# Laying the product rows of a state-space scan eight partitions apart, loaded in twelve transfers of 16 rows per chunk

## The reference

```python
xc = silu(conv(x_z)); dt = clip(softplus(xc @ dt_W + dt_b), 0.001, 0.1)
Bp = xc @ B_W; Cp = xc @ C_W; A = -exp(A_log)
def step(h, ins):
    x_t, dt_t, B_t, C_t = ins
    dA = exp(dt_t[..., None] * A)
    h = dA * h + dt_t[..., None] * B_t[:, None, :] * x_t[..., None]
    y_t = einsum('ben,bn->be', h, C_t)
```

## Time and profile before

| | us |
|---|---|
| median of 3 runs | 1180.5 (1174.55 to 1181.07) |
| profiled execution | 1172.6 |
| its span, first to last instruction | 1170.8 |
| staging part, then scan | to about 176, then to the end |
| TensorE / VectorE / ScalarE / GpSimd busy | 1018.2 / 937.3 / 910.6 / 851.4 |
| mean granted clock of TensorE | 0.905 of full |

### The profile page before, as it was taken

One profiled execution on the slowest core, in us unless ns is written; L12 is line 12 of the kernel. 1 busy time (PEld: TensorE's weight loads), 2 busy tenths in 40 slices (PEclk: granted clock), 3 DMA queues, 4 the chain that ended last, 5 costly groups with the idle time before them and its releaser, 6 DMA issues.

```text
span 1170.8 us, 27899 instructions
## 1 busy us (share of the span) xinstructions
PE 1018.2 (87%) x8006; PEld 433.0 (37%) x8006; DVE 937.3 (80%) x2127; ACT 910.6 (78%) x1093; POOL 851.4 (73%) x1218
## 2 busy tenths in 40 slices
PE   5988864899989999977999987999988999987997
PEld 3555521123433343423343433333332334332436
DVE  5667634889987998976998986997986998987983
ACT  1675656789988998877998886987986899887971
POOL 5465434788886888875888875887876888876880
PEclk9999985559997998997998987997988998998989
DMA  4243459999999999997999997999998899999930
GB/s 132 104 150 125 170 180 364 314 307 319 341 322 315 321 345 323 331 309 263 322 354 326 323 314 240 338 328 321 316 322 282 301 336 335 312 309 290 333 137 10
DMA packets 77141, 327.38 MB, mean 280 GB/s; under 512 B 13857, under 2 KB 33185, under 8 KB 41889
## 3 DMA queue, kind: packets, MB, share of 16 engines
q1 hardware_dynamic: 76960, 325.31, 82.9%
HBM read 303.24 MB, written 22.02 MB: 278 GB/s over the span
## 4 chain that ended last, share of the span: by engine, by line
PE 32%; DVE 17%; issue 11%; DMA 11%; POOL 8%; ACT 3%; SPq 2%; DVEq 1%; ACTq 0%; POOLq 0%
PE ps L985 12%; DMA decay<-dt_stage 11%; PE ps L930 7%; POOL decayed L876 7%; DVE ps L1193 7%; PE ps L1070 6%; DVE state L1204 5%; PE ps L1084 3%; ACT state L1132 2%; DVE h L1308 2%; DVE h L1317 1%; SPq L174 1%; SPq L800 1%; PE ps L1035 1%; ACT decay L1112 1%
## 5 line engine op out<-in xcount | busy, mean ns | idle before, releaser
L876 POOL TENSOR_TENSOR decayed<-decay,state 128x256 f32<-128x256 f32 x1024 | 726.1, 733 | 214.3 <-DVE state L1204 175.2
L1112 ACT ACTIVATE decay<-decay,a_col 128x2048 f32<-128x2048 f32 x256 | 512.8, 2003 | 68.0 <-DMA decay<-dt_stage 55.5
L1204 DVE TENSOR_TENSOR state<-decayed,ps 128x256 f32<-128x256 f32 x1024 | 398.8, 415 | 56.2 <-POOL decayed L876 28.4
L1193 DVE TENSOR_TENSOR ps<-decay,ps 128x512 f32<-128x512 f32 x512 | 352.2, 688 | 89.2 <-ACT state L1132 41.6
L985 PE MATMUL ps<-state,c_cols 128*32 128x256 f32 x4096 | 364.1, 431 | 0.0
L1132 ACT COPY state<-ps 128x512 f32<-128x512 f32 x512 | 289.7, 581 | 89.9 <-issue 46.8
L930 PE MATMUL ps<-moving,b_rows 36*128 36x256 bf16 x1024 | 215.9, 294 | 108.1 <-DVE ps L1193 103.8
L937 PE MATMUL ps<-moving,b_rows 36*128 36x256 bf16 x1024 | 217.4, 296 | 0.0
L1070 PE MATMUL ps<-h,w 128*128 128x256 f32 x512 | 189.9, 459 | 1.0 <-DVE h L1308 0.8
L930 PEld LDWEIGHTS ps<-moving,b_rows 36*128 36x128 bf16 x1024 | 59.0, 96 | 298.2 <-DVE ps L1193 180.1
L985 PEld LDWEIGHTS ps<-state,c_cols 128*32 128x32 f32 x4096 | 84.4, 113 | 123.8 <-issue 110.2
(11 more groups left out here) (119 smaller groups left out, 825.2 us busy)
## 6 DMA issues: line engine op xcount, KB each, us to landing
decay<-dt_stage SPq DMA_DIRECT2D x512, 512.0 KB, 7.8
moving<-u_stage SPq DMA_DIRECT2D x64, 288.0 KB
b_stage<-b_parts SPq DMA_DIRECT2D x24, 384.0 KB, 3.4
b_rows<-b_stage SPq DMA_DIRECT2D x128, 72.0 KB
dt_stage<-dt_tok SPq DMA_DIRECT2D x8, 512.0 KB, 3.1
u_stage<-u_parts SPq DMA_DIRECT2D x8, 512.0 KB, 2.8
x_tok<-in_L_attn_x_dram SPq DMA_DIRECT2D x4, 512.0 KB, 3.5
u_stage<-u_parts SPq DMA_DIRECT2D x8, 256.0 KB, 2.0
```

The lines of the kernel that those rows point to most:

```text
L876: nc.gpsimd.tensor_tensor(decayed[:, p], decay[:, dec_slot(m, k), p, k % TS, :], state[:, (k - 1) % RING, p * E:(p + 1) * E], ALU.mult).th ...
L1112: nc.scalar.activation(pair, pair, ACT.Exp, scale=a_col[:, 2:3]).then_inc(decay_ready, 1)
L1193: nc.vector.tensor_tensor(ps[:, acc_bank(m, k), :].rearrange("p (q e) -> p q e", q=HQ), decay[:, dec_slot(m, k), HQ:Q, k % TS, :], ps[:, a ...
L1204: nc.vector.tensor_tensor(state[:, k % RING, p * E:(p + 1) * E], decayed[:, p], ps[:, SELFP + k % 2, p * E:(p + 1) * E], ALU.add).then_inc ...
```

## The change

The row of part i of u and part j of B, for sequence b of pair hq in half f, moves to partition 64 f + 32 b + 8 i + 4 hq + j. In each half the rows of one (hq, j) then lie eight partitions apart, over all 128: 16 rows with the index (f, b, i), where i runs to SLOTS = 4, one more than there are parts. For the spare i the staged B rows are zero (two stores of zeros after the first sequence) and the staged u rows repeat the third part, so that product is zero. `load_u` and `load_b` take one hq and issue three transfers of 16 rows, one for each j; a chunk has 12 transfers in place of 6, six before and six behind the next four decay transfers. Matmuls contract 64 rows instead of 36. The staged tensors are laid out to match, with T + TC = 528 steps in a row instead of 512 (of which the last 16 are not used); the third part of u is stored twice. `moving` is cleared, half 0 on GpSimd, half 1 on VectorE, since partitions with remainder 3 and 7 by eight are never loaded. The waits on loads count 6 per buffer instead of 2 and 4.

```diff
-    u_stage = nc.dram_tensor("u_stage", (B, NP, T, E), BF16, kind="Internal").ap()
+    u_stage = nc.dram_tensor("u_stage", (HQ, HQ, 2, SLOTS, T + TC, E), BF16, kind="Internal").ap()
-    b_stage = nc.dram_tensor("b_stage", (B, NP, NP, T, 2 * N), BF16, kind="Internal").ap()
+    b_stage = nc.dram_tensor("b_stage", (HQ, NP, HQ, 2, SLOTS, T + TC, 2 * N), BF16, kind="Internal").ap()
...
-        def load_u(sp, t, cb):
-
-            for f in range(2):
-                r0 = f * HROW
-                sp.dma_start(moving[r0:r0 + UROWS, cb].rearrange("r t e -> r (t e)"),
-                             u_stage[f * HALF:(f + 1) * HALF, :, bass.ds(t, TC), :]
-                             .rearrange("b i t e -> (b i) (t e)")
-                             .unsqueeze(1).broadcast_to([HALF * NP, NP, TC * E])
+        def product_rows(hq, j):
+
+            return slice(hq * SLOTS + j, P, ESTEP)
+
+        def load_u(sp, t, cb, hq):
+
+            for j in range(NP):
+                sp.dma_start(moving[product_rows(hq, j), cb].rearrange("r t e -> r (t e)"),
+                             u_stage[hq, :, :, :, bass.ds(t, TC), :].rearrange("f b i t e -> (f b i) (t e)")
                              ).then_inc(chunk_loaded[cb], 16)
 
-        def load_b(sp, t, cb, pairs):
-
-            for pair in pairs:
-                r0 = (pair // HQ) * HROW + (pair % HQ) * PROWS
-                sp.dma_start(b_rows[r0:r0 + PROWS, cb, pair % HQ].rearrange("r t n -> r (t n)"),
-                             b_stage[2 * pair:2 * pair + 2, :, :, bass.ds(t, TC), :]
-                             .rearrange("b i j t n -> (b i j) (t n)")
+        def load_b(sp, t, cb, hq):
+
+            for j in range(NP):
+                sp.dma_start(b_rows[product_rows(hq, j), cb, hq].rearrange("r t n -> r (t n)"),
+                             b_stage[hq, j, :, :, :, bass.ds(t, TC), :].rearrange("f b i t n -> (f b i) (t n)")
                              ).then_inc(b_loaded[cb], 16)
...
+                        wait_all(sp, [(S["u_split"], n + 1)])
+                        sp.dma_start(u_stage[hq, f, bb, 2:4, 0:T].rearrange("i (p j) e -> p i (j e)", j=NJ),
+                                     u_parts[:, bb, 2].rearrange("p j e -> p (j e)").unsqueeze(1)
+                                     .broadcast_to([P, 2, NJ * E])
+                                     ).then_inc(S[f"parts_stored{bb}"], 16)
...
+                            if n == 0:
+                                sp.wait_ge(rows_zeroed, 2)
+                                zeros = b_rows[:, 0, 0].rearrange("p t n -> p (t n)")[:, 0:NJ * 2 * N].unsqueeze(1)
+                                for hq in range(HQ):
+                                    spare = b_stage[hq, :, :, :, SLOTS - 1, 0:T].rearrange("v f b t n -> (v f b) t n")
+                                    sp.dma_start(spare.rearrange("r (p j) n -> p r (j n)", j=NJ),
+                                                 zeros.broadcast_to([P, NP * HALF, NJ * 2 * N])
+                                                 ).then_inc(spare_stored, 16)
...
+                        nc.gpsimd.memset(moving[:, 0], 0.0)
                         nc.gpsimd.memset(b_rows[:, 0], 0.0).then_inc(rows_zeroed, 1)
...
+                        nc.vector.memset(moving[:, 1], 0.0)
                         nc.vector.memset(b_rows[:, 1], 0.0).then_inc(rows_zeroed, 1)
...
-            LOADS = 2
+            LOADS = NP * HQ
...
-                            load_u(sp, t0 + TC, 1)
-                            load_b(sp, t0 + TC, 1, range(0, 2))
+                            load_u(sp, t0 + TC, 1, 0)
+                            load_b(sp, t0 + TC, 1, 0)
                         next_dt(*range(TS, 5, TS))
                         if not first:
-                            load_b(sp, t0 + TC, 1, range(2, Q))
+                            load_u(sp, t0 + TC, 1, 1)
+                            load_b(sp, t0 + TC, 1, 1)
...
-                        return slice(f * HROW, f * HROW + UROWS)
+                        return slice(f * HROW, (f + 1) * HROW)
```

More of the change, by code:

```diff
@@ L46, in mamba_and_binary_mlp_block @@
     HROW = P // 2
-    PROWS = NP * NP * 2
-    UROWS = NP * NP * HALF
-    assert UROWS <= HROW
+    SLOTS = 4
+    ESTEP = P // (HALF * SLOTS)
+    ROWS = P // ESTEP
+    assert ESTEP == 2 * SLOTS and NP < SLOTS
     QE = Q * E
@@ L286, in _ @@
                     for cb in range(2):
-                        load_u(sp, cb * TC, cb)
-                        load_b(sp, cb * TC, cb, range(Q))
+                        for hq in range(HQ):
+                            load_u(sp, cb * TC, cb, hq)
+                            load_b(sp, cb * TC, cb, hq)
                     for bb in range(2):
@@ L847, in body @@
                             wait_all(sp, [(acc_state, t0 + TC + 1)])
[L848 to L849 removed]
+                            load_u(sp, t0 + STEPS, 0, 0)
+                            load_b(sp, t0 + STEPS, 0, 0)
                         next_dt(*range(16 + TS, 21, TS))
                         if not last:
[L852 removed]
+                            load_u(sp, t0 + STEPS, 0, 1)
+                            load_b(sp, t0 + STEPS, 0, 1)
                         next_dt(*range(20 + TS, STEPS + 1, TS))
```

24 lines of the change are left out of this document (12 added, 12 removed).

## The result

The changed kernel takes **1214.2 us** (median of 4 runs, 1210.5 to 1224.5) against 1177.5 us for the kernel before (the three runs above and a fourth, 1162.4 to 1181.1): a ratio of 1.0405, 95% interval 1.0339 to 1.0472. It is 4% slower, where 2% faster was forecast, and lies outside the range. The profiled execution took 1213.6 us, its span 1211.8 us, at a mean granted clock of 0.932.

The account below looks back on a forecast made before the run. No engine full: a chain over 512 time steps, with decay loads late because DMA is behind. 1172.6 us - 31 + 4 = 1145.6 us; the same 27 us off the median of 1180.5 give 1153.5 us, range 1128 to 1185.

Parts of the forecast that it names:

- The loss of a chunk's loads: DMA time lost per chunk behind u and B loads: 4.0 us before, taken to fall to 1.5, giving 31 us.
- the slack of 1.9 us: Per chunk, the other engines' 28.0 us against DMA's need of 26.1 us; the change was to make it 3.7 us.
- The bursts are also halved: Reason for the 31 us gain: 0.59 MB twice with four decay loads between, where 0.74 and 0.15 MB stood.
- bytes rule: Rival, chance 0.08: number of rows read sets the loss, 2.0 us more per chunk, 1231.5 us in all.
- Only the evenness changes: Rival, chance 0.13: 36 and 18 rows can't use all 16 DMA engines; busiest carries 1.4% less, 1176.5 us.
- SP's issue time: Before the scan, 24 loads at 0.40 us in place of 12: 2.4 us more, bounds for the 24 8.4 and 22.3.
- SP late: Rival, chance 0.05: each 16-row load costs SP 0.93 us, delaying decay loads, so nothing of 31 us is left: 1197.5 us.
- The first exponential: At the scan's start, waits 6.74 us for its load; set to come 1 us earlier, between -4 and +3.
- so their time stays: Product matmuls contracting 64 rows instead of 36, same 256 columns: no change in time.
- The cap of 44 us: Most the scan could gain if no decay load were late any more, between 40 and 48 us.
- a possible 12 us more: Extra gain if 20 chunks without a late load get 0.6 us each too; used for the range's lower end.
- the pitch may do nothing: Staged u rows 256 KiB apart, padded by 8 KiB: by one rule the loss would go altogether; the trace couldn't tell.

Follow-up runs that it names:

- side after side: Changed kernel with all six u loads ahead of the decay loads, partitions with remainder 0 to 3 by eight first, then 4 to 7: 1159.5 us, 0.9885.
- three u loads of 32 rows: Changed kernel, same partitions and bytes, u loads of both hq merged into three, four partitions apart, all ahead of the decay loads: 1108.5 us, 0.9525.
- in turn: Changed kernel with all six u loads ahead of the decay loads, first rows 0, 4, 1, 5, 2, 6: 1131.7 us, 0.9648.

## Why the prediction was wrong

The changed kernel can be put together from single steps on the kernel before. The loss per chunk is worked out as in the section on the result, over 29 chunks of each profiled execution; kernels that differ only in the padding of the staged rows lie within 0.3 us of each other in it. The times come from several sets of runs, so compare the ratios.

| kernel | us | ratio to before | a chunk, us | lost of it, us |
|---|---|---|---|---|
| before | 1173.5 | 1 | 29.95 | 6.2 |
| matmuls over 64 rows | 1165.5 | 0.9938 | 29.83 | 6.1 |
| and each chunk's loads split into two bursts, one half each | 1216.9 | 1.0371 | 31.65 | 8.1 |
| and rows eight apart, 12 loads, a third more bytes (the changed kernel) | 1214.2 | 1.0405 | 31.16 | 7.3 |
| the changed kernel, its second u burst moved ahead, side after side | 1159.5 | 0.9885 | 29.25 | 5.4 |
| three u loads of 32 rows | 1108.5 | 0.9525 | 27.78 | 4.0 |

The stretches of the second, third, fifth and sixth line:

```profile
217.69:1082.71 865.02, 750.75 (x6778) 300.06 (x6774) 740.65 (x1751) 729.03 (x881) 691.44 (x1015) 0.94 0.95 317
216.98:1134.93 917.95, 770.53 (x6778) 305.28 (x6774) 742.79 (x1751) 731.90 (x882) 691.66 (x1015) 0.92 0.96 299
224.33:1072.51 848.18, 746.56 (x6778) 299.36 (x6774) 739.83 (x1751) 731.47 (x882) 691.61 (x1015) 0.95 0.97 334
219.44:1025.10 805.66, 731.05 (x6782) 296.31 (x6782) 737.40 (x1752) 730.16 (x882) 691.52 (x1015) 0.98 0.97 351
```

**The loss of a chunk's loads: wrong.** "The rows lie nearer the lower end … I take a loss of 1.5 us", where 4.0 stood before. It measured 7.3 us, and 6.2 before: the loss did not fall, it grew. Rows that lie evenly over all partitions were taken for rows that reach all ports. The prediction named the port rule of the Trainium skill, saw that a new load reaches 8 of 16, and still let more than half of the loss go; but the old loads reached no more than 8 either. What the place of the rows is worth can be read between the third and fourth line, 8.1 to 7.3 us, and between the second and the fifth, 6.1 to 5.4: 0.7 to 0.8 us a chunk. The added bytes take 0.7 us at full rate, so nothing is left, and no clear difference in time (1.0371 and 1.0405, with overlapping intervals).

The loss before was read too low as well. The 4.0 us came from 8 us behind one burst, and the chunk's other slow stretches were left out. Over whole chunks the engines were busy 28.5 us and not 26.1, which is more than the 28.0 that the other engines were given: the slack of 1.9 us was not there.

**"The bursts are also halved": wrong, and the costliest line.** It stood there as a reason for the gain. The split is what made the kernel slower: 51 us in the table (6.1 to 8.1 us lost per chunk), and 4.4% with the old rows alone, where nothing else was changed. The prediction had priced the step by bytes, 0.59 and 0.59 MB. Price it by what runs at the same time instead. In the kernel before, the two u loads of a chunk follow each other and lie on different halves, so that part of the one can overlap with the other; split, each burst and the decay loads behind it queue at one set of ports. This reading fits the orders tried (side after side 1160, in turn 1132, all ports in each load 1108), but it is inferred: the trace doesn't show ports, and by themselves, without decay loads between, such pairs gained only 10 to 14% of rate (161 against 147, 227 against 200 GB/s).

**Bytes and the rival "bytes rule": nearest.** It stood at 0.08 and gave 1231.5 us. Its signs came, a rate near 200 GB/s behind the loads and more late decay loads (85 instead of 24). Its reason didn't: rows read are not what sets the loss (32 rows at 355 GB/s, 16 at 206). That it came within 18 us is luck.

**"Only the evenness changes."** Its assumption was right as far as the share of the engines shows (0.72 to 0.76 with 36 rows, 0.94 to 0.98 with 16), its time (1176.5) not: the engines are used more evenly, and the rate stays at half.

**SP's issue time: too small, and nearly harmless.** 24 x 0.40 us was 24 x 0.66, 8.6 us more than before where 2.4 were forecast, within its bounds. A load of 16 rows on separate partitions costs 0.62 us and not what 18 neighbouring rows do (0.39). The "SP late" rival fell all the same: six more small loads per chunk cost nothing, and the scan's start, made 7 us earlier, moved no end. The first exponential was not 1 us earlier but 6.3 us later, outside the -4 to +3.

**64-row matmuls "so their time stays": wrong.** The columns are the same, but the clock went from 0.905 to 0.941 with that step alone. It was worth 7 us here, the other way from the loss.

**The cap of 44 us: too low.** With 4.7 us of waits left the gain was 63 us, some 7 of them from the 64-row matmuls. The chunks that the prediction took as free of late loads, at 28.0 us, could gain too: with three u loads 29 chunks, those at the loop's edge included, take 27.78 us each. The prediction had this only as a possible 12 us more.

**Right.** That the pitch may do nothing was left open, and it does nothing; the figures that the prediction cited begin at 512 KiB, and the rows were 256 KiB apart. VectorE's memset took its 1.76 us and GpSimd's took 3.50 us, the latter hidden (it still idled 2.75 us for VectorE afterwards):

```profile
23.32 1.76 DVE L668 MEMSET moving<- 128x2048 uint32 x1 [0.38 <-issue]
```

```profile
18.75 3.50 POOL L380 MEMSET moving<- 128x4096 bf16 x1
...
28.45 0.20 POOL L330 TENSOR_TENSOR nrm<-mean_var,eps_t 128x4 f32<-128x4 f32 x1 [2.75 <-DVE mean_var L570]
```

The rate after a chunk's loads and ScalarE's waits for decay were the right places to look.

## What to carry to other kernels

Judge a row load by which partitions it reaches, not by whether its rows look evenly spread: eight apart over all 128 was half rate, four apart nearly full. Where loads can't reach everything, let those that follow each other closely reach different parts, and don't pull such a pair apart behind other loads, even if each burst gets smaller. Read what a group of loads loses over whole periods, as busy time less bytes at full rate, and not from the one slow stretch that caught the eye. Before a gain is booked for a new layout, ask whether the old one's loss had another cause than the one the new layout removes.

## What the runs showed of the hardware that was not expected

- With rows apart, SP's time to issue a load did not depend on their number: 16 loads of 16 rows eight apart took 10.04 us, of 32 rows four apart 10.02 us, of 64 rows two apart 10.16 us (0.63 us each). Of 32 neighbouring rows from one source row they took 7.28 us (0.46), of 18 neighbours of 4 KB 5.65 us (0.35), of 36 neighbours from 12 source rows 12.77 us (0.80).
- Contracting 64 rows instead of 36, the rest zero, raised the mean granted clock from 0.905 to 0.941 in otherwise the same kernel, and from 0.888 to 0.927 in the split one. No run tells why.
- ScalarE's waits for decay loads varied more than the time: 55.5 us in the kernel before, 40.7 with padded staged rows, 33.0 with six extra small loads, all within 0.3% of each other in time.
- Sides in turn brought 28 us in the kernel (1160 to 1132) and only 204 to 227 GB/s by themselves. What the decay loads in the queue add to this wasn't tried alone.
